# A change of index order inside the blocks of a long convolution: outer product and gated sum on one Trainium2 core

## The reference

```
v = layernorm(x)                      # (8, 256, 512)
vr, x1r, x2r = v, ctx, ctx            # each seen as (8, 32, 8, 512): 32 groups of 8 positions
kv = vr[:, :, :, None, :] * x2r[:, :, None, :, :]      # all pairs (i, j) of a group
y  = causal convolution of kv with k[h] along the last axis (512)   # by FFT of size 1024
y  = y + kv * skip[i]
out[b, h, j, :] = sum over i of y[b, h, i, j, :] * x1r[b, h, i, :]
x  = x + tanh(g_xattn[0]) * out
```

## Time and profile before

| | us |
|---|---|
| median of 3 runs (3468.52 to 3481.24) | 3470.72 |
| the profiled execution | 3481.24 |
| its span in the trace | 3479.4 |
| convolution, first product to last matmul | 97.94 to 383.08 |

### The profile page before, as it was taken

The page is one execution under the profiler, slowest core; times in us unless marked ns, Lnnn a source line. Parts: engine busy times, 40 slices in busy tenths (PEclk is TensorE's granted clock), DMA queues, the critical chain, the costliest instruction groups (busy, mean ns, idle before and its releaser), DMA issues.

```text
span 3479.4 us, 50524 instructions
## 1 busy us (share of the span) xinstructions
PE 2971.5 (85%) x18610; PEld 1731.8 (50%) x18610; DVE 2563.3 (74%) x4642; ACT 1631.9 (47%) x2565; POOL 926.6 (27%) x1309
## 2 busy tenths in 40 slices
PE   4899898884788888578888866999999999988998
PEld 2344566663344444256666633455445445444665
DVE  5699669999766666588888877777777777765333
ACT  3000144444355555138787884444544454454433
POOL 2566100000300000015566686222222222211000
PEclk7999999997899999799889978999999999999999
DMA  7233121211211010300000031000000000021000
GB/s 269 73 91 90 41 61 55 61 58 64 59 29 26 23 25 11 118 13 1 1 1 1 1 94 55 7 7 7 1 7 7 1 7 7 1 64 37 13 18 18
DMA packets 52646, 132.55 MB, mean 38 GB/s; under 512 B 6416, under 2 KB 19536, under 8 KB 51152
## 3 DMA queue, kind: packets, MB, share of 16 engines
q1 hardware_dynamic: 43216, 96.11, 9.2%
q10 hardware_dynamic: 9216, 33.56, 3.2%
HBM read 119.03 MB, written 4.19 MB: 35 GB/s over the span
## 4 chain that ended last, share of the span: by engine, by line
PE 51%; DVE 26%; issue 12%; ACT 8%; POOL 3%; DMA 1%; DVEq 0%; SPq 0%; POOLq 0%; ACTq 0%
PE psum L1089 10%; PE psum L517 8%; PE psum L1977 4%; PE psum L2544 3%; PE psum L2503 3%; PE psum L668 3%; PE psum L2528 2%; PE psum L2513 2%; PE psum L1991 2%; DVE area_c L2120 2%; ACT area_g L2067 2%; PE psum L1316 2%; PE psum L1335 2%; DVE area_a L1678 2%; DVE xn L2801 1%
## 5 line engine op out<-in xcount | busy, mean ns | idle before, releaser
L2067 ACT ACTIVATE area_g<-area_a 128x2048 bf16<-128x2048 f32 x156 | 310.6, 1995 | 47.2 <-DVE area_a L2138 30.2
L1977 PE MATMUL psum<-area_c,ident_bf 128*128 128x128 bf16 x3584 | 248.6, 234 | 96.0 <-DVE area_c L2120 95.9
L172 POOL TENSOR_TENSOR rstd<-mean_var,eps_col 128x2 f32<-128x2 f32 x65 | 20.7, 319 | 1089.5 <-DVE mean_var L590 564.3
L1977 PEld LDWEIGHTS psum<-area_c,ident_bf 128*128 128x128 bf16 x3584 | 231.6, 106 | 124.3 <-DVE area_c L2120 117.6
L517 PE MATMUL psum<-area_b,area_g 128*128 128x512 f32 x640 | 280.8, 602 | 4.6 <-DVE x_stream L455 3.1
L668 PE MATMUL psum<-xT_high,area_a 128*128 128x256 f16 x1024 | 239.4, 282 | 1.4 <-DVE xT_low L605 1.4
L668 PE MATMUL psum<-xT_low,area_a 128*128 128x256 f16 x1024 | 238.9, 281 | 0.0
L2503 PE MATMUL psum<-area_b,stage 128*128 128x512 f32 (+1 forms) x512 | 237.6, 546 | 0.0
L2794 DVE TENSOR_REDUCE small<-psum 128x1 f32<-128x384 f32 (+1 forms) x256 | 158.3, 618 | 71.9 <-PE psum L2504 70.7
L2655 ACT ACTIVATE xn<-psum,small 128x384 f32<-128x384 f32 (+1 forms) x256 | 163.6, 639 | 96.0 <-DVE small L2794 95.8
L2420 POOL TENSOR_TENSOR small<-small,half_pow 128x4 f32<-128x4 f32 x96 | 131.6, 1371 | 273.9 <-DVE small L2741 273.9
(11 more groups left out here) (407 smaller groups left out, 7655.9 us busy)
## 6 DMA issues: line engine op xcount, KB each, us to landing
stage<-in_w ACTq DMA_DIRECT2D x24, 512.0 KB, 4.4
stage<-in_w SPq DMA_DIRECT2D x24, 512.0 KB, 3.6
area_g<-in_toeplitz SPq DMA_DIRECT2D x32, 256.0 KB, 2.6
area_b<-in_ctxT SPq DMA_DIRECT2D x15, 512.0 KB, 4.0
area_b<-area_b SPq DMA_DIRECT2D x24, 256.0 KB, 3.7
stage<-in_ctxT SPq DMA_DIRECT2D x9, 512.0 KB, 4.0
x_stream<-in_x SPq DMA_DIRECT2D x4, 1024.0 KB, 8.9
area_c<-in_ctxT SPq DMA_DIRECT2D x4, 1024.0 KB, 15.5
```

Source lines behind the costliest of these rows:

```text
L1977: last = nc.tensor.matmul(psum[:, 1, t_ * P:(t_ + 1) * P], identb[:, :], above5[:, t_, c * P:(c + 1) * P], start=(c == 0), stop=(c == KE - 1))
L2067: nc.scalar.activation(junk5[t_], z5[b % 3][:, t_, :], ACT.Sign, bias=fine5[:, par, t_:t_ + 1], scale=-1.0, accum_out=signs5[:, t_:t_ + 1] ...
```

## The change

In both instructions the two inner indices of the 512 columns change places. Before, a block of 64 columns was ordered (j, i) with i innermost; now it is (i, j) with j innermost. GpSimd still writes `kv` without gaps; which input repeats one element and which runs over eight is swapped. TensorE's instructions are untouched: the same products over columns in another order. VectorE reads PSUM without gaps as before, repeats each context element eight times in a row in place of running over eight, and writes `tmp` in its old order (b, j, i), so that the sum after it is the same instruction as before; the write therefore goes in steps of 8 elements (32 bytes).

```diff
                         nc.gpsimd.tensor_tensor(
-                            kv[:, par, k, :].rearrange("p (b j i) -> p b j i", b=B, i=HW),
-                            vT[:, k, :, cols].unsqueeze(2).broadcast_to([P, B, HW, HW]),
-                            cT[:, k, :, cols].unsqueeze(3).broadcast_to([P, B, HW, HW]), ALU.mult).then_inc(sig("kv_ready"), 1)
+                            kv[:, par, k, :].rearrange("p (b i j) -> p b i j", b=B, i=HW),
+                            vT[:, k, :, cols].unsqueeze(3).broadcast_to([P, B, HW, HW]),
+                            cT[:, k, :, cols].unsqueeze(2).broadcast_to([P, B, HW, HW]), ALU.mult).then_inc(sig("kv_ready"), 1)
...
                     nc.vector.tensor_tensor(
-                        tmp.rearrange("p (b j i) -> p b j i", b=B, i=HW),
-                        psum[:, 4 * par + m, :].rearrange("p (b j i) -> p b j i", b=B, i=HW),
-                        cT[:, m, :, cols].unsqueeze(2).broadcast_to([P, B, HW, HW]), ALU.mult).then_inc(sig("y_drained"), 1)
+                        tmp.rearrange("p (b j i) -> p b i j", b=B, i=HW),
+                        psum[:, 4 * par + m, :].rearrange("p (b i j) -> p b i j", b=B, i=HW),
+                        cT[:, m, :, cols].unsqueeze(3).broadcast_to([P, B, HW, HW]), ALU.mult).then_inc(sig("y_drained"), 1)
```

## The result

The changed kernel takes 3499.6 us (median of 6 runs, 3492.9 to 3508.3) against 3471.7 us (6 runs) for the kernel before. That is 28 us more; 38 were forecast. Over all 23 runs of the changed kernel on record, whose median is 3500.4 us, the ratio is 1.0083, 95% interval 1.0069 to 1.0096, or 24 to 33 us. The profiled execution is one of 3496.7 us with a span of 3494.9.

The account below looks back on a forecast made before the run. TensorE was taken to bound the convolution, with VectorE close behind; slower L464 stores make VectorE the bound, +37.2 us over its cycles plus 1.2 ahead, about +38: 3470.7 to 3509 us, 8-in-10 range 3465 to 3530, forecast's own 3488 to 3530.

Parts of the forecast that it names:

- TensorE bounds the stage, VectorE stands next to it: Convolution: TensorE busy 200.00 of 200 us, half-step 8.583 us; VectorE busy 184.83, without visible slack in 24 of 32 half-steps.
- GpSimd and the inner repeat cost nothing: GpSimd's multiply L426 with exchanged inputs, and L464's context element read eight times in a row: 0 us each.
- The store costs, x = 0.60 us: VectorE's L464 storing 512 elements 32 bytes apart: x, its gain per instruction, taken as 0.60 us, making it 1.28 us.
- rival B: A small price on VectorE's L464 store, x of 0.21 to 0.41 us: about +10, 3481 us; chance 0.12.
- The reading of the 16-element copy: Small copy to places 128 bytes apart, 196 ns, used as upper bound for L464's store: x = 0.45 or 0.72 us.
- The memsets: Small memsets with elements 128 bytes apart, 0.81 ns per element against 0.83 adjacent: lower bound for L464's store, x = 0.
- The sum 7.73 + 4x: VectorE's cycle per half-step with weights: 7.73 us plus four L464 gains, 10.13 us, 1.55 over TensorE's 8.583.
- The cheap ternary pair throughout: VectorE's ternary pair, clear of GpSimd's multiplies, costs 2.11 us in place of 2.97; only the first two half-steps pay 0.85 more.
- my own sum: Convolution stage: 24 cycles with weights, 3 without, plus 1.7 us: 268.9 against 231.7, with 1.2 us ahead +38 us.
- The clock: TensorE's granted clock may fall through its stops: at 0.90 nothing lost, at 0.80 +58 us; chance 0.06, shared with a high price.

Follow-up runs that it names:

- e1: Only GpSimd's L426 in the new index order, VectorE's L464 old, against the kernel before (output not the reference's): 3466.6 us, ratio 0.9994.
- e5: Changed kernel with the 24 weight-chunk loads issued by ScalarE in place of SyncE: 3491.3 us, ratio 1.0060 to the kernel before.
- e4: Changed kernel, but VectorE's product reads PSUM in steps of 32 bytes and writes without gaps: ratio 1.0005 to the kernel before.
- e9: Changed kernel, but only blocks 0 and 1 of each half-step store in 32-byte steps; 2 and 3 read PSUM in steps: 3470.6 us, ratio 0.9997.

## Why the prediction was right, and what was off

- **TensorE bounds the stage, VectorE stands next to it:** right; with the change VectorE is the bound, and the timeline shows it.
- **GpSimd and the inner repeat cost nothing:** right (e1; L3057 against L3056, 691 ns each).
- **The store costs, x = 0.60 us:** right in sign, too large. It is 0.394, which belongs to rival B's band of 0.21 to 0.41. The reading of the 16-element copy carried the error: it gave 0.9 to 1.4 ns per element, while 512 of them pay 0.77. Two reasons are at hand, and no run tells them apart: a duration of 16 elements is mostly its fixed part, so that I may have read a slope out of a difference of fixed parts; and that copy is of float16 elements and was set against float32 ones, two types that pay very differently when stored 16 bytes apart (2400 ns in L3065, 1064 in L3059). The memsets gave the right slope, which holds even for 512 elements, though L1702 writes runs of eight words rather than all adjacent ones (L437, without gaps, takes the same 165 ns). But a memset is no model for an instruction that also reads: it pays nothing where a copy pays.
- **The sum 7.73 + 4x:** exact where it applies, 9.31 us per cycle from 171.50 to 218 us, and in e5 between 252.69 and 261.98 (9.29).
- **The cheap ternary pair throughout:** this term failed. Over the 24 pairs the cycles of the change cost 12.5 us more than the cheap form would. The sum had 1.7 us of this for the first two, which measured 1.5. It had nothing for the rest, and two things are in it. The three pairs from 218.08 on cost 2.7 us: the sum lets the lag grow to 12 us and did not ask what the pair passes on the way, and it is GpSimd's next four multiplies. The 14 pairs from 248.73 on cost 8.3 us: I let TensorE be held by the banks alone and did not ask what stands in SyncE's queue, where the Toeplitz slice is issued behind a wait on the ternary pair. e5, which takes that wait out of the way, still pays the first part (2.8 us) and none of the second, and its stage is 8.0 us shorter.
- So for x = 0.394 my own sum gives +16 us, and rival B's +10 for x = 0.34 was too low as well; the 11 us of pairs that the sum left out bring it to 27, where 28 were measured. The forecast of 38 had a price 50% too high (22 us) and a term of 11 us missing. That 3499.6 us lies inside the forecast's own range of 3488 to 3530 is partly luck: x itself lies in rival B's band, and with the price alone put right the sum would have said 3487 us. The two errors have opposite signs.
- **The clock:** no loss, as predicted; 1.00 in the window in spite of 14 us of stops.
- Not settled: why the lag locks where it does with the late slice. Shown is that TensorE starts right behind the landing of the slice, and that with the pair in its old place the stops shrink and the pair gets cheap when the slice has a queue of its own. That it is GpSimd's multiplies that stretch the pair is read from the coincidence in time in the traces; no run takes GpSimd away.

Nothing tried beats the kernel before by more than its interval. e4 and e9 equal it.

## What to carry to other kernels

When a permutation of float32 has to be made somewhere, put it on VectorE's PSUM side (free here in steps of 32 bytes), or keep runs of two adjacent float32 on the SBUF side. An engine with no idle time may still have slack if its instructions run longer beside another engine's: compare the durations with the same forms elsewhere in the trace. And follow every queue that feeds the bound engine for a wait on the engine you make slower; a DMA issued behind such a wait inherits its lag.

## What the runs showed of the hardware that I had not expected

- A float16 store of single elements 16 bytes apart took 2400 ns for 512 elements (L3065), against 1064 for float32 at the same distance (L3059) and 682 for a float16 difference stored in runs of 16 adjacent elements elsewhere in the kernel (L1640). I did not follow this up.
- A memset pays nothing for single elements 32 bytes apart (485 ns for 512), while a copy does (1072 ns).
- VectorE's PSUM reads in steps of 32 bytes are free (692 against 691 ns), and SBUF reads are not (1065).
